# Two-layer graph network on one core: ScalarE fetches one subtile of every four groups row by row, and VectorE adds a finished block behind the fourth tile's messages

## What is computed

```python
h = maximum(layernorm(x), 0)                       # layer 1: attention over the edges, 8 heads of 16
z = h @ W;  el, er = z . attn_l, z . attn_r
a = exp(leaky_relu(el[src] + er[dst]) - emax[dst])
x = x + segment_sum(z[src] * a, dst) / segment_sum(a, dst) + bias
h = maximum(layernorm(x), 0)                       # layer 2: messages weighted by a small network
s, v = h[:, :32] @ W_up_s, h[:, 32:] @ W_up_v      # one scalar and one 3-vector per channel
w0, w1, w2, w3 = silu(silu(edge_feats @ A1 + b1) @ A2 + b2) @ A3
message = segment_sum([s[src]*y_s*w0, (v[src].y_v)*w3, s[src]*y_v*w1, v[src]*y_s*w2], dst) / 10
x = x + message @ W_out
```

## Time and profile before

| what | value |
|---|---|
| median of 3 runs | 3959.68 us |
| the profiled execution | 3959.96 us, its span 3958.1 us |
| busy share of the span: PE, DVE, ACT, POOL | 66%, 63%, 25%, 74% |
| granted TensorE clock, whole span | 0.81 of full speed |
| chain that ended last | POOL 43%, issue 21%, PE 12%, DVE 8%, DMA 7% |
| gathers of GpSimd | 1539 in each layer |

### The profile page before, as it was taken

The page is one execution under the profiler, slowest core; times in us unless marked ns, Lnnn a source line. Parts: engine busy times, 40 slices in busy tenths (PEclk is TensorE's granted clock), DMA queues, the critical chain, the costliest instruction groups (busy, mean ns, idle before and its releaser), DMA issues.

```text
span 3958.1 us, 64895 instructions
## 1 busy us (share of the span) xinstructions
PE 2594.4 (66%) x11162; PEld 1893.4 (48%) x11163; DVE 2490.1 (63%) x6074; ACT 1006.3 (25%) x1440; POOL 2913.5 (74%) x3088
## 2 busy tenths in 40 slices
PE   3545455545555555555578878787888888888887
PEld 2444444444444444444445555555555555555554
DVE  7444444444444444444467878887888878887787
ACT  4333333333333333333331111111111111111111
POOL 2777777777777777777767777777777777777776
PEclk8666666666666666666679999999999999999999
DMA  4222222222222222222212222222222222222221
GB/s 130 63 63 62 63 62 62 62 62 62 62 62 62 62 63 63 62 61 63 62 50 59 62 59 62 59 62 59 62 61 60 59 62 62 59 59 63 61 60 53
DMA packets 150584, 248.11 MB, mean 63 GB/s; under 512 B 59341, under 2 KB 97335, under 8 KB 150167
## 3 DMA queue, kind: packets, MB, share of 16 engines
q0 software_dynamic: 98496, 214.52, 21.8%
q1 hardware_dynamic: 51642, 30.27, 2.9%
q10 hardware_dynamic: 144, 0.80, 0.1%
HBM read 235.33 MB, written 10.03 MB: 62 GB/s over the span
## 4 chain that ended last, share of the span: by engine, by line
POOL 43%; issue 21%; PE 12%; DVE 8%; DMA 7%; SPq 5%; DVEq 1%; ACT 0%; POOLq 0%; ACTq 0%
POOL rows L485 43%; PE pair L1401 5%; PE pair L1322 5%; SPq L402 4%; DMA rows<-up_tab,idx 4%; DMA rows<-z_tab,idx 3%; DVE share L1044 2%; SPq L398 1%; PE pair L1358 1%; DVE share L1162 1%; DVE share L1158 1%; DVE acc L935 1%; PE pair L1348 1%; DVE share L1156 0%; PE pair L1352 0%
## 5 line engine op out<-in xcount | busy, mean ns | idle before, releaser
L485 POOL DMA_INDIRECT rows<-z_tab,idx x1539 | 1459.9, 949 | 539.9 <-issue 513.4
L485 POOL DMA_INDIRECT rows<-up_tab,idx x1539 | 1452.1, 944 | 487.3 <-issue 445.6
L1322 PE MATMUL pair<-share,acc 128*128 128x136 f32 x3126 | 750.3, 431 | 806.2 <-DVE share L1044 806.2
L1322 PEld LDWEIGHTS pair<-share,acc 128*128 128x128 f32 x3126 | 695.7, 324 | 939.9 <-DVE share L1044 937.9
L1401 PE MATMUL pair<-share,acc 128*128 128x256 f32 x3126 | 795.8, 399 | 295.2 <-DVE share L1167 291.7
L1401 PEld LDWEIGHTS pair<-share,acc 128*128 128x128 f32 x3126 | 574.9, 193 | 664.8 <-DVE share L1167 567.0
L1033 DVE TENSOR_TENSOR share<-rows,share 128x64 f32<-128x64 f32 x196 | 44.4, 226 | 855.6 <-DMA rows<-z_tab,idx 824.3
L1358 PE MATMUL pair<-weights_sb,share 128*128 128x256 f32 x1568 | 390.8, 394 | 30.5 <-ACT acc L641 29.1
L1155 DVE TENSOR_TENSOR share<-rows,pair 128x384 f32<-128x384 f32 x391 | 216.3, 553 | 302.2 <-DMA rows<-up_tab,idx 282.5
L628 ACT ACTIVATE share<-pair,front_sb 128x512 f32<-128x512 f32 x196 | 134.6, 687 | 927.0 <-PE pair L1348 927.0
L1358 PEld LDWEIGHTS pair<-weights_sb,share 128*128 128x128 f32 x1568 | 307.7, 199 | 84.1 <-issue 39.5
(11 more groups left out here) (168 smaller groups left out, 2384.8 us busy)
## 6 DMA issues: line engine op xcount, KB each, us to landing
rows<-z_tab SPq DMA_DIRECT2D x3072, 0.6 KB
rows<-up_tab SPq DMA_DIRECT2D x3072, 0.5 KB
rows<-z_tab,idx POOLq DMA_INDIRECT x1539
rows<-up_tab,idx POOLq DMA_INDIRECT x1539
ef_sb<-in_edge_f SPq DMA_DIRECT2D x50, 128.0 KB
z_tab<-rows SPq DMA_DIRECT2D x7, 504.0 KB, 3.2
y_sb<-in_edge_y SPq DMA_DIRECT2D x50, 64.0 KB
x_sb<-in_x SPq DMA_DIRECT2D x7, 448.0 KB, 7.0
```

Source lines behind the costliest of these rows:

```text
L485: pool.indirect_dma_start(out=to[:, t, 0:width], out_offset=None, in_=table, in_offset=bass.IndirectOffsetOnAxis(ap=indices[:, t:t + 1], a ...
L1322: mm = t.matmul(bank[2 + h][:, 0:MW], hot[:, s, i, :], msg[:, h, i, :], start=(i == 0), stop=(i == tiles - 1))
```

## The change

1. **ScalarE fetches a subtile.** In every fourth group (f = 3) the first subtile of slot 2 is no longer gathered by GpSimd. ScalarE fetches its 128 rows one by one, spread over the 13 tiles before: `fetch_ahead` reads 12 or 8 row numbers into registers and issues a direct DMA for each (STEPS: 12 in tiles 0 and 2 of a group, 8 in tiles 1 and 3; the 13th step, in tile 0 of group f = 3, is of 8). In layer 1 the step stands behind the tile's line 584 (line 603 of the changed kernel), in layer 2 behind its line 630 (line 666) and, in tile 2, ahead of the block's three copies.
2. **Columns.** `rows` has a further column, `ahead`, between slots 1 and 2; slots 2 and 3 lie one column further on. To make room in SBUF, `w_aug` and `ones_row` are now laid over memory that is used later.
3. **Loops.** `groups4` writes four groups into a body that runs 12 times, for GpSimd, ScalarE and VectorE. TensorE and SyncE keep theirs.
4. **VectorE in layer 2** adds the finished block behind the messages of tile 3 (line 1129 there), no longer behind tile 2's sums.
5. **Start.** Ahead of its first pass ScalarE waits until the row numbers of the single fetches are in SBUF (`loads["single"]`).

```diff
+STEPS = (12, 8) * 6 + (8,)
...
+        rows_all = sb("rows", [P, U * T + 2, ZW])
+        ahead = rows_all[:, 2 * T, :]
+        single = rows_all[:, U * T + 1, :]
...
+        def groups4(eng, body):
+            with eng.Fori(0, GI // 4) as w:
+                for f in range(4):
+                    body(w * 4 + f, w * 2 + f // 2, f % 2, w, f)
+            body(GI - 1, GI // 2, 0, GI // 4, 0)
...
                     def four_tiles(q, r, e, w=None, f=0):
...
-                            short, fetched = isinstance(r, int) and s == U - 1, e == 1 and s == U - 1
-                            gather(slot_rows(s, fetched), idx[:, e, s, :], tab, width,
-                                   (s_l1["rows0"][s], s_l1["rows1"][s]), LT if short else T - 1 if fetched else T)
+                            short, beside = isinstance(r, int) and s == U - 1, e == 1 and s == U - 1
+                            in_front = f == 3 and s == 2
+                            gather(slot_rows(s, beside or in_front), idx[:, e, s, :], tab, width,
+                                   (s_l1["rows0"][s], s_l1["rows1"][s]), 1 if in_front else 0,
+                                   LT if short else T - 1 if beside else T)
...
+            def fetch_ahead(tab, width, w, step, fetched):
+                first = sum(STEPS[:step])
+                _, nodes = nc.values_load_multi_w_load_instructions(
+                    ahead_i[0:1, bass.ds(w * P + first, STEPS[step])], engines=(mybir.EngineType.Activation,), min_val=0,
+                    max_val=NODES - 1, skip_runtime_bounds_check_because="they are sources, below NODES")
+                for i, node in enumerate(nodes):
+                    act.dma_start(ahead[first + i:first + i + 1, 0:width], tab[bass.ds(node, 1), 0:width])\
+                       .then_inc(fetched, 16)
+
+            act.wait_ge(s_in["stored_early"], 16 * REUSED)
+            act.wait_ge(s_in["stored"], 16 * (BI - REUSED))
+            act.wait_ge(loads["single"], 16)
...
+                        if not isinstance(r, int) and f * U + s < len(STEPS):
+                            fetch_ahead(z_tab, ZW, w, f * U + s, s_l1["ahead"])
+                        if f == 3 and s == 3:
+                            hold(act, s_l1["msg1"][2], n)
...
+                        if not isinstance(r, int) and f * U + s < len(STEPS):
+                            fetch_ahead(up_tab, HIDDEN, w, f * U + s, s_l2["ahead"])
+                        if f == 3 and s == 3:
+                            hold(act, s_l1["msg0"][2], n_2)
                         if s == 2:
                             hold(act, s_l1["added"][0], n)
                             blocks(act, mybir.EngineType.Activation, q + 1, stage_block)
...
-                        if over:
-                            blocks(dve, mybir.EngineType.DVE, GI, add_block)
-                        else:
+                        if s == U - 1:
+                            blocks(dve, mybir.EngineType.DVE, q + 1, add_block)
+                        if not over:
                             one_hot2((s + 1) % U, q * U + (s + 1))
...
                         add_sums2((s - 1) % U, low[s], high[s])
-                        if s == 2 and not isinstance(r, int):
-                            blocks(dve, mybir.EngineType.DVE, q + 1, add_block)
```

More of the change, by code:

```diff
@@ L54 @@
 LW = ZW + HEADS
-assert 0 < LT < HT and GI % 2 == 1 and QUADS <= 64 and AHEAD == 2 and U == 4
+assert 0 < LT < HT and GI % 4 == 1 and sum(STEPS) == P and QUADS <= 64 and AHEAD == 2 and U == 4
 assert NB == BU * BI and NG == U * GI and NG * GE >= EDGES and PAD_DST >= NODES + 3 * P and WIN + HALF - 1 <= P
@@ L310, in groups, with slot_rows, landed_ahead @@
             body(GI - 1, GI // 2, 0)
+        def groups4(eng, body):
[3 more added lines that the diff above has]
+            body(GI - 1, GI // 2, 0, GI // 4, 0)
         IN2 = 16 * (GI + 1) // 2
         SETS = GI + 1
-        ROWS_IN = {"rows0": [GI * 16 * HT] * (U - 1) + [(GI - 1) * 16 * HT + 16 * LT],
-                   "rows1": [GI * 16 * HT] * (U - 1) + [(GI - 1) * 16 * HT - GI // 2 * 16]}
+        ROWS0 = {"up": [GI * 16 * HT] * 2 + [GI * 16 * HT - GI // 4 * 16, (GI - 1) * 16 * HT + 16 * LT]}
+        ROWS0["z"] = ROWS0["up"]
+        ROWS1 = [GI * 16 * HT] * (U - 1) + [(GI - 1) * 16 * HT - GI // 2 * 16]
         FETCHED = 16 * P
-        def slot_rows(s, fetched):
-            return moved_on if fetched and s == U - 1 else rows[:, s, :, :]
+        def slot_rows(s, fetched=False):
+            at = s * T + s // 2
+            if fetched:
+                at += 1 if s == U - 1 else -1
+            return rows_all[:, at:at + T, :]
+        def landed_ahead(w, f):
+            return w * (64 * HT - 16) + (16 * HT * (f + 1) - f // 3 * 16)
         def landed_beside(r, e):
@@ L405, in _ @@
             sp.wait_ge(G["columns_set"], 1)
-            sp.dma_start(single_i, src_single).then_inc(loads["single"], 16)
+            sp.dma_start(singles_i, src_single).then_inc(loads["single"], 16)
             sp.wait_ge(s_in["stored_early"], 16 * REUSED)
@@ L481, in _, with gather @@
             pool.memset(minus_id, 0.0).then_inc(zeroed, 1)
-            def gather(to, indices, table, width, done, n=T):
-                for t in range(n):
+            def gather(to, indices, table, width, done, first=0, last=T):
+                for t in range(first, last):
                     pool.indirect_dma_start(out=to[:, t, 0:width], out_offset=None, in_=table,
@@ L497, in _, with gather_edges @@
                     hold(pool, s_max["idx"], g + 1)
-                    gather(rows[:, 0, :, :], idx_max, z_tab, ZW, (s_max["rows"],) * 2)
+                    gather(slot_rows(0), idx_max, z_tab, ZW, (s_max["rows"],) * 2)
                 hold(pool, s_max["free"], NG + 1)
-            def gather_edges(tab, width, before, rows_stored):
+            def gather_edges(tab, width, before, rows_stored, landed0):
                 with pool.Fori(0, passes1) as k:
@@ L619, in four_tiles @@
                         set_idx(e, q * U + 2 * U)
-                groups(act, four_tiles)
+                groups4(act, four_tiles)
                 first_idx()
@@ L1018, in four_tiles @@
                         ts = slice(0, LT if last and s == U - 1 else T)
-                        rows_s = slot_rows(s, e == 1)
+                        in_front = f == 3 and s == 2
+                        rows_s = slot_rows(s, in_front or e == 1 and s == U - 1)
                         el_e = rows_s[:, ts, MW:ZW]
                         if last and s == U - 1:
-                            dve.wait_ge(s_l1["rows0"][s], ROWS_IN["rows0"][s])
+                            dve.wait_ge(s_l1["rows0"][s], ROWS0["z"][s])
                         else:
-                            dve.wait_ge(s_l1["rows0"][s], landed)
+                            if s == 2:
+                                dve.wait_ge(s_l1["rows0"][s], ROWS0["z"][s] if last else landed_2)
+                            else:
+                                dve.wait_ge(s_l1["rows0"][s], landed)
+                            if in_front:
+                                dve.wait_ge(s_l1["ahead"], fetched_2)
                             dve.wait_ge(s_l1["rows1"][s], landed_3 if s == U - 1 else landed)
```

79 lines of the change are left out of this document (46 added, 33 removed).

## The result

The changed kernel takes **4009.5 us** (median of 4 runs, 4008.8 to 4018.6) where the kernel before takes 3960.5 beside it: 1.0128 times as long, 95% interval 1.0115 to 1.0142. It is slower by some 49 us (1.3%). The forecast was 3936.3, with a range of 3929 to 3966. The profiled execution took 4008.81 us, its span 4006.7, at a mean granted clock of 0.77 in place of 0.81.

A forecast was written before the change was run, and what follows sets the result against it. The prediction took GpSimd's gathers, 1.248 us each, as the bound. It summed 3959.96 - 30.0 (24 gathers fewer) + 0.3 (start) + 6 (layer 2's clock loss) = 3936.3 us, range 3929 to 3966.

The forecast's parts named there:

- The clock takes that: Layer 2: TensorE's room of only 5 us in GpSimd's 156 is used up by a lower clock after idling.
- If each long group loses these 1.9 us once: Layer 2, groups f = 0 to 2: low clock makes four groups 156.5 us, 6 us lost in 12 turns.
- Layer 2 goes over to TensorE and ScalarE: Rival: layer 2's chain through ScalarE's step in tile 2 outlasts the gathers; 4004 us with doubled clock loss; chance 0.17.
- the slack is 12.8: Argument against the slower layer 2 rival: GpSimd's wait for TensorE's sums passes 12.8 us ahead.
- 24 gathers less at 1.248 us: GpSimd issues 12 gathers fewer in each layer, saving 30.0 us if it stays the bound.
- A step of 12 takes 6.3 us, one of 8 takes 4.5: ScalarE's sequencer time per fetch step, from 0.43 us a DMA and 1.1 us a register load.
- Layer 1 costs nothing, the start 0.3 us (bounds 0 and 2): Layer 1's steps fit into existing room, cost 0; ScalarE's later first passes at the start cost 0.3 us.
- A long group without the clock's loss, 39.3 us: Layer 2, a group with a step of 12 ahead of tile 2's block: 39.3 us on TensorE.
- The group f = 3, 33.0: Layer 2, the group with no step ahead of its block: 33.0 us if TensorE is never early.
- VectorE's add moves at no cost, "without a wait": Layer 2: the add behind tile 3's messages gains 0 in itself and no longer waits for the block.
- Loops of four groups cost 0: Each of ScalarE's 24 loop turns may cost 2.8 us of code fetch, which falls into slack: 0.
- The gathers slow down: Rival: a third DMA issuer adds 0.01 us to each of 3054 gathers, giving 3960 us; chance 0.03.

The follow-up runs named there:

- e_layer1_alone: The change kept in layer 1 only; in layer 2 ScalarE fetches nothing and GpSimd gathers all rows: 3946.6 us, ratio 0.9967.
- e_add_back: The changed kernel with VectorE's add of layer 2 back at its old place, ahead of tile 3's messages: 4025.9 us, ratio 1.0177.
- e_none_in_tile2: The changed kernel with the same 128 DMAs in layer 2, but none ahead of the block in tile 2: 3935.7 us, ratio 0.9936.
- e_behind_block: The changed kernel with layer 2's step of tile 2 moved from ahead of the block to behind it: 3932.2 us, ratio 0.9930.
- e_warm: The changed kernel with 28 unused TensorE transposes ahead of its wait in tile 2 of groups f = 0 to 2: 4012.7 us, ratio 1.0133.
- e_six_in_tile2: The changed kernel with layer 2's steps 12, 10, 6, 12 in groups f = 0 to 2 and 8 in f = 3: 3942.1 us, ratio 0.9955.
- e_eight_in_tile2: The changed kernel with layer 2's steps 8, 12, 8, 12 in groups f = 0 to 2 and 8 in f = 3: 3951.7 us, ratio 0.9984.
- e_warm_24: The changed kernel with layer 2's steps 8, 4, 24, 4 (8 in f = 3) and 101 transposes in tile 2: 4098.3 us, ratio 1.0338.

## Why the prediction was wrong

**The step that failed** is "The clock takes that": "If each long group loses these 1.9 us once". The mechanism, its place and its sign were right; the size was off. The term was taken from one stretch of sixteen sums. After the change the low clock lies over the mapping, a radial stretch, hidden1 and half of the sums, and costs 5.1 us. A long group then takes 8.0 + 7.3 + 21.7 + 7.3 = 44.3 us where 41.2 were forecast, and as a mean over all (some have no block, in 10 of 30 the clock comes back sooner) 42.9. A turn has 162.0 in place of 156.5. At 12 turns the forecast's 6 us become 71 by the turns, 77 by the gathers. The stated upper bound was 74, and it was put down as the rival "Layer 2 goes over to TensorE and ScalarE", 4004 us with a chance of 0.17. That is what happened. Its argument "the slack is 12.8" does not help against it: slack is spent once, and the excess of 5.9 us comes in each of 12 turns; no part of the 71 us was taken up. With only 5 us of room in 156 and a price of 36 times each microsecond, a chance of 0.17 looks small for a clock loss that had been read from one stretch of one layer.

The Trainium skill warns of this (TensorE: Matmul & The Clock Gate, HAM oscillation — how this bites in real kernels): where TensorE waits in each turn of a loop, the clock falls in each and the work behind the wait starts slow. The trace agrees: the clock falls in all 30 long groups of the table, from 1.00 before the wait to 0.50 behind it.

Point by point:
- *24 gathers less at 1.248 us:* right. 1527 a layer at a median of 1.249.
- *A step of 12 takes 6.3 us, one of 8 takes 4.5:* 5.9 and 4.1. The DMAs come every 0.394 us, not 0.43; the loads are 0.56 to 0.97. A small error to the safe side.
- *Layer 1 costs nothing, the start 0.3 us (bounds 0 and 2):* one stall of 1.5 us at 107 us, then nothing. The layer ends 13.3 us sooner, and e_layer1_alone gained 13.3 on the kernel before beside it.
- *A long group without the clock's loss, 39.3 us:* right to 0.1. With the clock held up it is 8.0 + 7.3 + 16.6 + 7.3 = 39.2. Two errors cancel in it: an even tile takes 8.0 and not 7.62, because the step of 12 keeps the next tile's first silu waiting (missed), and a tile with the step of 8 takes 7.29.
- *The group f = 3, 33.0:* 33.2.
- *VectorE's add moves at no cost, "without a wait":* the first is right (e_add_back is 16 us slower), the second wrong. It waits up to 8.4 us, for VectorE has done tile 3's messages by 3384 and the block is moved at 3392.
- *Loops of four groups cost 0:* right, by e_none_in_tile2 and e_behind_block, which have them with all the DMAs and 4 and 1 us of waiting.
- *The gathers slow down:* no; the pace is unchanged in layer 2 with a third issuer.

## What to carry to other kernels

When a wait of some microseconds is put in front of TensorE, price the low clock over everything that TensorE does behind it until the clock is back, at the durations of the lower level for each stretch; here it nearly doubled the delay. When two engines' totals are within a few per cent (150.9 against 156.0), give the slower outcome a chance by the worst reading of each term times the number of repeats. And put work that nobody waits for behind the instruction that another engine waits for: moving twelve DMAs behind the block's three small copies was worth 77 us.

## What the runs showed of the hardware that was not expected

- The same idle time does not always cost the same. In e_warm TensorE idled 3.75 us in one long group and the clock was at 0.50 before the radial began; in another it idled 3.62 us and the clock fell only behind the mapping: low for 13.7 and for 3.4 us, 21.9 and 17.95 us for the tile. e_six_in_tile2 and e_eight_in_tile2 have the block equally late (6.1 us) and lie 10 us apart: in 3 and in 13 of their 30 long groups the clock is low for 13.7 us.
- TensorE's clock can be kept up by transposes of a constant: 60 of them, 6.71 us in each long group, held it at 1.00 and are worth 74 us of the kernel's time.
- A register load on ScalarE does not cost by its count alone: 12 numbers from a multiple of four took 0.8 to 0.97 us, 8 took 0.56 to 0.73 and 10 took 1.2, but 6 (from place 22) took 1.5 and 11 (from place 29) took 2.4. No run separates the count from the place. The Trainium skill gives a floor (DMA: Bandwidth & Descriptors, Latency and other measured facts) of some 600 ns. Loads of 4 numbers took 0.32 to 0.51 us here (e_warm_24), so the measurement decides.
